# Attention projections of a two-layer transformer kernel in three full blocks, with moved odd heads and transposed values

## The chip, the core and the metric

The kernel runs on one core of a Trainium2 chip. The metric is the time of one execution on the device, in microseconds (us); lower is better. The engines are TensorE (PE, with its weight loads as PEld), VectorE (DVE), ScalarE (ACT), GpSimd (POOL) and SyncE (SP), which issues DMAs here.

## What is computed

x holds 32 batches of 256 tokens with 256 features. A first layer passes each batch through an expert of a conditional feed-forward, then attention, then a top-2 mixture of 8 experts; a second layer follows (base projection with LoRA, shared and routed experts). The change lies in the attention:

```python
def _gqa(x, wq, wk, wv, wo):                      # x is RMS-normed
    q = (x @ wq.T).reshape(B, S, N_HEADS, HEAD_DIM)      # 16 heads of 16
    k = (x @ wk.T).reshape(B, S, N_KV_HEADS, HEAD_DIM)   # 4 heads
    v = (x @ wv.T).reshape(B, S, N_KV_HEADS, HEAD_DIM)   # 4 heads
    k, v = jnp.repeat(k, n_rep, axis=2), jnp.repeat(v, n_rep, axis=2)
    attn = jnp.einsum('bqhd,bkhd->bhqk', q, k) * scale
    attn = jax.nn.softmax(jnp.where(causal, attn, -jnp.inf), axis=-1)
    out = jnp.einsum('bhqk,bkhd->bqhd', attn, v).reshape(B, S, C)
    return out @ wo.T
```

## The kernel before

The kernel is a row of phases: the conditional feed-forward (to about 330 us), the attention with the routing (to about 1055), the sorted experts, LoRA and shared experts, top-k and the routed experts. The engines meet through semaphores only; each engine's list is written out by hand and runs in order.

`attention_phase` runs `body(i)` once per batch on each engine, i from -3 to 31, with a loop of four bodies for batches 8 to 27. A body holds work of several batches: normalised rows of batch i + 3, projections of batch i + 2 (keys, values, queries), scores for the row maxima of batch i + 1, turned scores and exponentials of batch i, the output of batch i - 1 and the residual, the router's logits (`gate`) and, in even iterations, the prefix sums of batches before that (`prefix`).

Every fp32 product is made of three, from high and low parts (`exact_product`, L59 to L61). The projections write two PSUM banks. `piece_a` and `piece_b` are each shared by a fixed ring of users (`A_ORDER`, `B_ORDER`): the user named next may start when the one before it has been emptied, counted in `a_free` and `b_free`. For this change: `piece_b` goes from `kv` to `route` to `shift_q1` to `out_t`; `piece_a` from `heads_q1` to `q_a` to `q_b` to `values_q0`.

Queries and keys lie transposed: `q_t` has 128 partitions, 32 for each of four key groups, and four columns of heads j. Of each 32 rows row 0 holds the shift (minus the maximum, written there by SP with `move_shift`), rows 1 to 16 the head, the rest zeros. `k_t` is laid out alike, with ones in row 0, so that a product of 32 rows gives score minus maximum. The padding makes the queries four blocks of 128 weight columns and the keys a fifth. Each block takes 2 x 3 products over 256 tokens. The values are made untransposed, with tokens on the partitions: 8 products of 128 or 64 columns with `wv`.

In an iteration TensorE goes: turned scores 0, output projection, `turn_max` 0, scores 0, transposes of the norm, values of q1, turned scores 1, transposes of h, `heads` 0, scores 1, `heads` 1, `keys_values`, `queries` q_a, turned scores 2, (`prefix`), `gate`, `queries` q_b, `turn_max` 1 (L1600), scores 2, `turn_out`, values of q0. VectorE takes the maxima of each score bank (L1043), and `divide` frees piece_a for the queries. `keep_kv` copies keys and values (L1079, L1082) out of piece_b, and `keep_q` the first query block. ScalarE takes exponentials (L926), and its `keep_q` copies the second query block.

## Time and profile before

| | |
|---|---|
| median of 3 runs | 2264.63 us (2261.69 to 2268.38) |
| the profiled execution | 2275.81 us |
| its span | 2274.2 us |
| TensorE busy over the span | 2108.6 us (93%) |
| VectorE busy | 1372.2 us (60%) |
| ScalarE busy | 1113.6 us (49%) |
| GpSimd busy | 972.6 us (43%) |

The page has one profiled execution. A busy TensorE is not TensorE at its peak: matmuls are pipelined, and in the order of time the start of the next instruction, not the length of one, says how fast the list goes. An idle stretch stands in square brackets with what ended it.

### The profile page before, as it was taken

How to read it: one execution, taken by the hardware profiler on the slowest of the kernel's cores; microseconds unless marked ns; L12 is line 12 of the kernel's file. 1: busy time of each engine (PE TensorE's matmuls, PEld its weight loads, DVE VectorE, ACT ScalarE, POOL GpSimd, SP SyncE). 2: the span in 40 equal slices, each digit the busy share in tenths (PEclk: the TensorE clock that was granted, in tenths of full speed). 3: DMA queues.
4: the chain of work that ended last, by engine and by line, in shares of the span. 5: the costliest groups of instructions: out<-in, count | busy, mean ns of one | idle time of the engine just before them, and what ended most of it. 6: DMA issues, size and time to landing. Idle time of an engine off the chain costs nothing. (4 is left out here: it accounts for less than half of the span.)

```text
span 2274.2 us, 51155 instructions
## 1 busy us (share of the span) xinstructions
PE 2108.6 (93%) x16904; PEld 1793.8 (79%) x16904; DVE 1372.2 (60%) x2834; ACT 1113.6 (49%) x2206; POOL 972.6 (43%) x1062
## 2 busy tenths in 40 slices
PE   5999978999999999997997999999839999999997
PEld 5999975666666666664996999999828888888886
DVE  5888854576666766676553666666554544444442
ACT  5666643455555555554663333333224544445442
POOL 0000012244554545544654454545235566655653
PEclk9999988999999999997997999999969999999998
DMA  6666630221221212213985444444224545455442
GB/s 229 236 236 237 240 116 25 99 72 63 85 81 62 83 60 86 80 54 110 310 294 172 135 152 137 150 141 149 84 92 105 106 98 115 90 109 108 95 88 31
DMA packets 127209, 285.06 MB, mean 125 GB/s; under 512 B 20705, under 2 KB 58338, under 8 KB 120674
## 3 DMA queue, kind: packets, MB, share of 16 engines
q1 hardware_dynamic: 77026, 173.04, 23.1%
q0 software_dynamic: 50048, 110.14, 19.2%
q8 instruction: 94, 1.54, 0.3%
q14 instruction: 41, 0.34, 0.0%
HBM read 187.17 MB, written 95.42 MB: 124 GB/s over the span
## 5 line engine op out<-in xcount | busy, mean ns | idle before, releaser
L1043 DVE TENSOR_REDUCE neg_max<-ring 128x2 f32<-128x512 f32 (+1 forms) x384 | 251.0, 680 | 109.1 <-PE ring L1554 109.1
L814 POOL TENSOR_SCALAR_AFFINE_SELECT weights_diag<-weights_diag 128x512 f32<-128x512 f32 x256 | 155.7, 633 | 323.5 <-ACT weights_diag L926 322.6
L2584 POOL DMA_INDIRECT out<-eo,row_put x128 | 201.2, 1572 | 162.7 <-ACT eo L2649 138.0
L2724 DVE TENSOR_TENSOR ex_hid<-ex_up_ps,gelu 128x512 f32<-128x512 f32 x128 | 86.9, 688 | 173.8 <-ACT gelu L2633 173.8
L2574 POOL DMA_INDIRECT toks<-hs,row_get x128 | 134.8, 1053 | 133.1 <-DVE row_get L2690 97.2
L2021 POOL DMA_INDIRECT picked_rows<-results,lo_row_now x128 | 145.8, 1139 | 56.5 <-issue 29.3
L2633 ACT ACTIVATE gelu<-ex_gate_ps 128x512 f32<-128x512 f32 x128 | 76.2, 596 | 188.7 <-PE ex_up_ps L61 188.7
L926 ACT ACTIVATE weights_diag<-ring 128x512 f32<-128x512 f32 x256 | 138.4, 599 | 35.7 <-PE ring L1570 35.7
L59 PE MATMUL ex_down_ps<-ex_dn_lo,ex_hid_hi 128*128 128x256 f32 x512 | 144.2, 282 | 2.8 <-issue 2.8
L311 POOL DMA_DIRECT2D c<-c_sb x31 | 17.0, 549 | 303.4 <-DVE c_sb L377 303.4
L61 PE MATMUL ex_down_ps<-ex_dn_hi,ex_hid_hi 128*128 128x256 f32 x512 | 143.8, 281 | 0.0
L60 PE MATMUL ex_down_ps<-ex_dn_hi,ex_hid_lo 128*128 128x256 f32 x512 | 143.7, 281 | 0.0
L822 POOL DMA_INDIRECT sorted_rows<-h_sb,row_now x128 | 127.1, 993 | 34.7 <-issue 32.0
L926 ACT ACTIVATE weights_full<-ring 128x512 f32<-128x512 f32 x128 | 67.3, 602 | 127.3 <-PE ring L1570 127.3
L1570 PE MATMUL ring<-q_t,k_t 32*128 32x512 f32 x768 | 112.1, 654 | 14.2 <-DVE neg_max L1043 9.5
L1550 PE MATMUL ring<-k_t,q_t 32*128 32x128 f32 (+1 forms) x2048 | 114.2, 349 | 11.9 <-issue 5.2
L59 PE MATMUL ps_up<-x_lo,ug_hi 128*128 128x256 f32 x256 | 76.3, 298 | 35.7 <-DVE ug_lo L343 22.1
L2068 ACT ACTIVATE ht_hi<-turned 128x512 fp32r<-128x512 f32 x32 | 19.1, 598 | 183.8 <-PE turned L2289 183.8
L1550 PEld LDWEIGHTS ring<-k_t,q_t 32*128 32x128 f32 x2048 | 81.6, 190 | 34.0 <-issue 28.1
L2717 DVE TENSOR_TENSOR ex_xt_lo<-ex_turned,ex_xt_hi 128x512 fp32r<-128x512 f32 x64 | 41.3, 686 | 110.3 <-ACT ex_xt_hi L2627 110.3
L59 PE MATMUL ex_gate_ps<-ex_xt_lo,gu_hi 128*128 128x512 f32 x256 | 104.3, 407 | 1.5 <-DVE ex_xt_lo L2717 1.5
L60 PE MATMUL ex_gate_ps<-ex_xt_hi,gu_lo 128*128 128x512 f32 x256 | 101.4, 396 | 0.0
(366 smaller groups left out, 7731.6 us busy)
## 6 DMA issues: line engine op xcount, KB each, us to landing
ug_raw<-in_w_ug SPq DMA_DIRECT2D x32, 1028.0 KB, 5.0
dn_raw<-in_w_dn SPq DMA_DIRECT2D x32, 640.0 KB, 6.2
q_t<-sorted_rows SPq DMA_DIRECT2D x136, 128.0 KB, 3.3
expert_gu<-in_expert_gu SPq DMA_DIRECT2D x16, 1024.0 KB, 4.8
results<-c0n POOLq DMA_DIRECT2D x33, 256.0 KB
x_raw<-in_x_t SPq DMA_DIRECT2D x32, 256.0 KB, 5.2
c0n<-c SPq DMA_DIRECT2D x32, 256.0 KB, 3.9
c0r<-c SPq DMA_DIRECT2D x32, 256.0 KB
```

The source lines that it names most:

```text
L59: nc.tensor.matmul(out, lhs_hi, rhs_lo, start=start, stop=False)
L60: nc.tensor.matmul(out, lhs_lo, rhs_hi, start=False, stop=False)
L61: return nc.tensor.matmul(out, lhs_hi, rhs_hi, start=False, stop=stop)
L814: nc.gpsimd.affine_select(part, part, [[0, G], [1, P]], ALU.is_ge, 0.0, base=0, channel_multiplier=-1).then_inc(kept_done, 1)
L822: nc.gpsimd.indirect_dma_start(out=sorted_rows, out_offset=to, in_=h_sb[b[1] % 4][:, t, :], in_offset=None).then_inc(scattered[b[1] % 2], 16)
L926: nc.scalar.activation(tile[:, g, :], slot(2 * r, g)[:], ACT.Exp).then_inc(exp_done, 1)
L1043: nc.vector.tensor_reduce(out, src, AX_X, ALU.max, negate=True).then_inc(max_done, 1)
L1550: nc.tensor.matmul(slot(2 * r + 1, g)[:, c * keys:(c + 1) * keys], q_t[n][rows, j, q * P:(q + 1) * P], k_t[n][rows, 0:keys], start=(c == 0 ...
L1570: nc.tensor.matmul(slot(2 * r, g)[:], k_t[n][rows, k * P:(k + 1) * P], q_t[n][rows, :, q * P:(q + 1) * P], start=True, stop=True).then_inc ...
L2021: nc.gpsimd.indirect_dma_start(out=picked[par][:, n, :], out_offset=None, in_=results, in_offset=bass.IndirectOffsetOnAxis(ap=row_now[par] ...
L2574: nc.gpsimd.indirect_dma_start(out=toks[c][:, n, :], out_offset=None, in_=hs_rows, in_offset=bass.IndirectOffsetOnAxis(ap=at, axis=0)).the ...
L2584: nc.gpsimd.indirect_dma_start(out=out_rows, out_offset=bass.IndirectOffsetOnAxis(ap=at, axis=0), in_=eo[c][:, n, :], in_offset=None, comp ...
```

## The change

The padding goes. The two heads of a pair share a block: rows 0 to 15 of each 32 hold an even head, rows 16 to 31 the odd one, so the queries are two blocks, and the third block holds the keys (rows 0 to 15) and the values (rows 16 to 31).

- ScalarE copies the query bank into the even columns of `q_t`. SP then moves the odd heads with four DMAs from rows 16 to 31 of the even columns to rows 0 to 15 of the odd ones (`move_odd_heads`), and `scores` of the next iteration waits for them. Later the shift is written to row 16 instead of row 0, over the old odd heads.
- ScalarE copies keys and values to `kv_t` in SBUF (`take_kv`). VectorE makes `k_t` from it (times 1 for key rows, plus 1 in row 16, with `of_key`). TensorE turns `kv_t` with two transposes into piece_b (`turn_v`), and VectorE copies the values out (`keep_v`). `v_t` is a new user of piece_b between `kv` and `route`.
- `queries` runs once and is one user of piece_a. The block that stood between `gate` and `turn_max` 1 is gone.
- `scores` uses 16 rows of each group, the turned scores 17. The maps of weights change to fit, and the sorted phase gets two buffers of its own for the parts that lay in the wider weight tiles.

```diff
-VW = NKV * HD
+HALF = 2 * HD
+KV = G // 2
...
-        self.wqk_raw = sb("wqk_raw", [P, KT, G + 1, P])
-        self.wqk_hi = sb("wqk_hi", [P, KT, G + 1, P], F32R)
-        self.wqk_lo = sb("wqk_lo", [P, KT, G + 1, P], F32R)
-        self.wv_raw = sb("wv_raw", [P, KT, VW])
-        self.wv = sb("wv", [P, KT, 2 * VW], F32R)
+        self.wqk_raw = sb("wqk_raw", [P, KT, KV + 1, P])
+        self.wqk_hi = sb("wqk_hi", [P, KT, KV + 1, P], F32R)
+        self.wqk_lo = sb("wqk_lo", [P, KT, KV + 1, P], F32R)
+        self.of_key = sb("of_key", [P, 2])
...
-                    nc.scalar.activation(at.wqk_hi[:, t, 0:G], at.wqk_raw[:, t, 0:G], ACT.Copy, scale=at.norm_q[:, t:t + 1]).then_inc(at.w_hi_done, 1)
-                    nc.scalar.activation(at.wqk_hi[:, t, G], at.wqk_raw[:, t, G], ACT.Copy, scale=at.norm[:, t:t + 1]).then_inc(at.w_hi_done, 1)
-                    nc.scalar.activation(at.wv[:, t, 0:VW], at.wv_raw[:, t], ACT.Copy, scale=at.norm[:, t:t + 1]).then_inc(at.w_hi_done, 1)
+                    nc.scalar.activation(at.wqk_hi[:, t, 0:KV], at.wqk_raw[:, t, 0:KV], ACT.Copy, scale=at.norm_q[:, t:t + 1]).then_inc(at.w_hi_done, 1)
+                    nc.scalar.activation(at.wqk_hi[:, t, KV], at.wqk_raw[:, t, KV], ACT.Copy, scale=at.norm[:, t:t + 1]).then_inc(at.w_hi_done, 1)
...
-        A_ORDER = (("out_proj", -2, B), ("values_q1", -1, B), ("heads_q0", -1, B), ("heads_q1", -1, B), ("q_a", 2, B), ("q_b", 2, B), ("values_q0", 0, B))
-        B_ORDER = (("shift_q0", 0, B), ("norm_t", 2, B), ("h_t", -2, B), ("kv", 2, B), ("route", -2, B + 1), ("shift_q1", 1, B), ("out_t", -1, B))
+        A_ORDER = (("out_proj", -2, B), ("values_q1", -1, B), ("heads_q0", -1, B), ("heads_q1", -1, B), ("q", 2, B), ("values_q0", 0, B))
+        B_ORDER = (("shift_q0", 0, B), ("norm_t", 2, B), ("h_t", -2, B), ("kv", 2, B), ("v_t", 2, B), ("route", -2, B + 1), ("shift_q1", 1, B), ("out_t", -1, B))
...
             def move_shift(b, q):
                 sp.wait_ge(b_free, per_b(f"shift_q{q}", later(b, -q)) + 1)
-                sp.dma_start(q_t[b[1] % 4][0:P:32, :, q * P:(q + 1) * P], shift[q][:]).then_inc(shift_in[q], 16)
+                sp.dma_start(q_t[b[1] % 4][HD:P:32, :, q * P:(q + 1) * P], shift[q][:]).then_inc(shift_in[q], 16)
+
+            def move_odd_heads(i):
+                n = (i[1] + 2) % 4
+                sp.wait_ge(a_free, per_a("q", i) + 1)
+                for g in range(NKV):
+                    sp.dma_start(q_t[n][32 * g:32 * g + HD, 1:G:2, :], q_t[n][32 * g + HD:32 * g + HALF, 0:G:2, :]).then_inc(odd_heads_in, 16)
...
                 if exists(later(i, 4)):
                     load_to_normalise(later(i, 4))
+                if exists(later(i, 2)):
+                    move_odd_heads(i)
                 if exists(later(i, 1)):
                     move_shift(later(i, 1), 1)
...
             def keep_q(i):
-                act.wait_ge(queries_done, times(2, i, 6))
-                nc.scalar.activation(q_t[(i[1] + 2) % 4][:, 2:4, :], piece_a[:].rearrange("p (j s) -> p j s", j=2), ACT.Copy).then_inc(a_free, 1)
+                act.wait_ge(queries_done, times(1, i, 3))
+                nc.scalar.activation(q_t[(i[1] + 2) % 4][:, 0:G:2, :], piece_a[:].rearrange("p (j s) -> p j s", j=2), ACT.Copy).then_inc(a_free, 1)
+
+            def take_kv(i):
+                act.wait_ge(kv_done, times(1, i, 3))
+                until(act, k_t_done, times(1, i, 2))
+                until(act, v_t_done, times(1, i, 2))
+                nc.scalar.activation(kv_t[:], piece_b[:, 0:S], ACT.Copy).then_inc(b_free, 1)
...
                     exps(i, 2, (0, 1))
                 if even(i) and exists(later(i, -4)):
                     second_odds(later(i, -4))
+                if has_next:
+                    take_kv(i)
                 if has:
                     exps(i, 2, (2, 3))
+                if has_next:
+                    keep_q(i)
                 if exists(later(i, 1)):
                     keep_shift(i)
...
-            def keep_kv(i):
-                n = (i[1] + 2) % 4
-                dve.wait_ge(kv_done, times(1, i, 3))
-                nc.vector.tensor_scalar(k_t[n][:], piece_b[:, 0:S], one_rows[:], None, ALU.add)
-                both = piece_b[:, S:512].rearrange("p (t a g d) -> p t g d a", t=TT, a=2, g=NKV)
-                for t in range(TT):
-                    part = nc.vector.tensor_reduce(v[n][:, t, :, 0:HD], both[:, t], AX_X, ALU.add)
-                part.then_inc(b_free, 1)
-
-            def keep_q(i):
-                dve.wait_ge(queries_done, times(2, i, 5))
-                nc.vector.tensor_copy(q_t[(i[1] + 2) % 4][:, 0:2, :], piece_a[:].rearrange("p (j s) -> p j s", j=2)).then_inc(a_free, 1)
+            def keep_k(i):
+                dve.wait_ge(b_free, per_b("kv", i) + 1)
+                nc.vector.scalar_tensor_tensor(out=k_t[(i[1] + 2) % 4][:], in0=kv_t[:], scalar=at.of_key[:, 0:1], in1=at.of_key[:, 1:2].broadcast_to([P, S]),
+                                               op0=ALU.mult, op1=ALU.add).then_inc(k_t_done, 1)
+
+            def keep_v(i):
+                dve.wait_ge(v_t_done, times(1, i, 3))
+                nc.vector.tensor_copy(v[(i[1] + 2) % 4][:, :, :, 0:HD],
+                                      piece_b[:, 0:S].rearrange("p (t g c) -> p t g c", t=TT, g=NKV)[:, :, :, HD:HALF]).then_inc(b_free, 1)
...
                     maxima(s, 1, 1)
-                if has_next:
-                    keep_kv(i)
                 if picks:
                     scaled_gap(m_pick)
-                if has_next:
-                    keep_q(i)
                 if has_scores:
                     maxima(s, 1, 2)
+                if has_next:
+                    keep_k(i)
+                if has_scores:
                     maxima(s, 1, 3)
+                if has_next:
+                    keep_v(i)
...
                     ring_free(times(12, i, 12), times(12, i, 2))
-                    until(pe, b_free, per_b("kv", later(i, -1)) + 1)
+                    until(pe, k_t_done, times(1, i, 2))
+                    pe.wait_ge(odd_heads_in, times(16 * NKV, i, 2 * 16 * NKV))
                 elif r == 1:
                     ring_free(times(12, i, 16), times(12, i, 6))
-                    until(pe, a_free, per_a("q_b", later(i, -1)) + 1)
...
-                        rows = slice(32 * g, 32 * g + 32)
+                        rows = slice(32 * g, 32 * g + HD)
...
-                    rows = slice(32 * g, 32 * g + 32)
+                    rows = slice(32 * g, 32 * g + HD + 1)
...
             def keys_values(i):
                 take_b("kv", i)
                 for k in range(KT):
-                    exact_product(nc, piece_b[:, 0:S], (at.wqk_hi[:, k, G, :], at.wqk_lo[:, k, G, :]),
-                                  (nt_hi[:, k, :], nt_lo[:, k, :]), k == 0, k == KT - 1)
+                    last = exact_product(nc, piece_b[:, 0:S], (at.wqk_hi[:, k, KV, :], at.wqk_lo[:, k, KV, :]),
+                                         (nt_hi[:, k, :], nt_lo[:, k, :]), k == 0, k == KT - 1)
+                last.then_inc(kv_done, 1)
+
+            def turn_v(i):
+                take_b("v_t", i)
                 for t in range(TT):
-                    toks = slice(t * P, (t + 1) * P)
-                    c = S + t * 2 * VW
-                    beside(piece_b[:, c:c + 2 * VW], VW, (nt_hi, nt_lo), toks, at.wv, True)
-                    last = beside_last(piece_b[:, c:c + 2 * VW], VW, (nt_hi, nt_lo), toks, at.wv)
-                last.then_inc(kv_done, 1)
+                    last = nc.tensor.transpose(piece_b[:, t * P:(t + 1) * P], kv_t[:, t * P:(t + 1) * P], at.ident[:])
+                last.then_inc(v_t_done, 1)
...
-            def queries(i, name, heads_):
-                take_a(name, i)
-                for c, j in enumerate(heads_):
+            def queries(i):
+                take_a("q", i)
+                for c in range(KV):
                     for k in range(KT):
-                        last = exact_product(nc, piece_a[:, c * S:(c + 1) * S], (at.wqk_hi[:, k, j, :], at.wqk_lo[:, k, j, :]),
+                        last = exact_product(nc, piece_a[:, c * S:(c + 1) * S], (at.wqk_hi[:, k, c, :], at.wqk_lo[:, k, c, :]),
                                              (nt_hi[:, k, :], nt_lo[:, k, :]), k == 0, k == KT - 1)
                 last.then_inc(queries_done, 1)
...
                     keys_values(i)
-                    queries(i, "q_a", (0, 1))
+                    queries(i)
                 if has:
                     turned_scores(i, 2)
+                if has_next:
+                    turn_v(i)
                 if picks:
                     prefix(i)
                 if has_h:
                     gate(i, not picks)
-                if has_next:
-                    queries(i, "q_b", (2, 3))
...
-    q_rows = np.zeros((G, NKV, 32, D), np.float32)
-    q_rows[:, :, 1:HD + 1] = a[F0 + "wq"].reshape(NKV, G, HD, D).swapaxes(0, 1)
-    k_rows = np.zeros((1, NKV, 32, D), np.float32)
-    k_rows[0, :, 1:HD + 1] = a[F0 + "wk"].reshape(NKV, HD, D)
+    q_rows = a[F0 + "wq"].reshape(NKV, KV, HALF, D).swapaxes(0, 1)
+    kv_rows = np.concatenate([a[F0 + "wk"].reshape(1, NKV, HD, D), a[F0 + "wv"].reshape(1, NKV, HD, D)], 2)
+    in_block = np.arange(P) % 32
...
-        "w_qk": by_rows(np.concatenate([q_rows, k_rows], 0).reshape(-1, D)).reshape(P, KT, G + 1, P),
-        "w_v": by_rows(a[F0 + "wv"]).reshape(P, KT, VW),
+        "w_qk": by_rows(np.concatenate([q_rows, kv_rows], 0).reshape(-1, D)).reshape(P, KT, KV + 1, P),
+        "of_key": np.stack([in_block < HD, in_block == HD], 1).astype(np.float32),
```

TensorE's list, an odd iteration, from the third turned scores on, before (nine more products of the second query block and then the transposed maxima, L1600, follow the last row):

```order
L1570 MATMUL ring<-q_t,k_t 128x512 x3
L1644 MATMUL piece_b<-gate,at_ht_hi 128x16 [waits b_free]
L1645 MATMUL piece_b<-gate,at_ht_lo 128x8
L1649 MATMUL piece_b<-gate,at_ht_lo 128x8
L1650 MATMUL piece_b<-gate,at_ht_hi 128x16
L1644 MATMUL piece_b<-gate,at_ht_hi 128x16
L1645 MATMUL piece_b<-gate,at_ht_lo 128x8
L1649 MATMUL piece_b<-gate,at_ht_lo 128x8
L1650 MATMUL piece_b<-gate,at_ht_hi 128x16
L59 MATMUL piece_a<-nt_lo,wqk_hi 128x256 [waits a_free]
L60 MATMUL piece_a<-nt_hi,wqk_lo 128x256
L61 MATMUL piece_a<-nt_hi,wqk_hi 128x256
```

and after the change:

```order
L1583 MATMUL ring<-q_t,k_t 128x512 x3
L1653 MATMUL piece_b<-at_ident,kv_t 128x128 [waits b_free]
L1653 MATMUL piece_b<-at_ident,kv_t 128x128
L1658 MATMUL piece_b<-gate,at_ht_hi 128x16 [waits b_free]
L1659 MATMUL piece_b<-gate,at_ht_lo 128x8
L1663 MATMUL piece_b<-gate,at_ht_lo 128x8
L1664 MATMUL piece_b<-gate,at_ht_hi 128x16
L1658 MATMUL piece_b<-gate,at_ht_hi 128x16
L1659 MATMUL piece_b<-gate,at_ht_lo 128x8
L1663 MATMUL piece_b<-gate,at_ht_lo 128x8
L1664 MATMUL piece_b<-gate,at_ht_hi 128x16
L1613 MATMUL piece_b<-at_ident,neg_max 16x128 [waits max_done,b_free]
```

The second query block is gone from between the gate's products and the transposed maxima, and two transposes of kv_t stand before the gate, which now waits for them to leave the bank.

ScalarE's list in the same place, before, from the exponentials of the third turned scores (weights_full) on:

```order
L926 ACTIVATE weights_full<-ring 128x512 [waits at_turned_done0]
L926 ACTIVATE weights_full<-ring 128x512 [waits at_turned_done1]
L926 ACTIVATE weights_full<-ring 128x512 [waits at_turned_done2]
L926 ACTIVATE weights_full<-ring 128x512 [waits at_turned_done3]
L954 ACTIVATE shift<-piece_b 16x128 [waits max_t_done]
L950 ACTIVATE q_t<-piece_a 128x512 [waits queries_done]
```

and after:

```order
L937 ACTIVATE weights_full<-ring 128x512 [waits at_turned_done0]
L937 ACTIVATE weights_full<-ring 128x512 [waits at_turned_done1]
L967 ACTIVATE kv_t<-piece_b 128x256 [waits v_t_done,k_t_done,kv_done]
L937 ACTIVATE weights_full<-ring 128x512 [waits at_turned_done2]
L937 ACTIVATE weights_full<-ring 128x512 [waits at_turned_done3]
L961 ACTIVATE q_t<-piece_a 128x2x256 [waits queries_done]
L971 ACTIVATE shift<-piece_b 16x128 [waits max_t_done]
```

The copy to kv_t came in behind the second exponential, and the copy to q_t, which now takes the even columns, stands ahead of the shift.

VectorE's list in the same place, before, from the second maximum of the second score set on:

```order
L1043 TENSOR_REDUCE neg_max<-ring 128x2 [waits scores_done]
L1079 TENSOR_SCALAR k_t<-piece_b,one_rows 128x256 [waits kv_done]
L1082 TENSOR_REDUCE v<-piece_b 128x4x16 x2
L1087 COPY q_t<-piece_a 128x512 [waits queries_done]
L1043 TENSOR_REDUCE neg_max<-ring 128x2 [waits scores_done] x2
L1158 TENSOR_REDUCE logits<-piece_b 128x16 [waits gate_done]
```

and after:

```order
L1062 TENSOR_REDUCE neg_max<-ring 128x2 [waits scores_done] x2
L1097 SCALAR_TENSOR_TENSOR k_t<-kv_t,of_key 128x256 [waits b_free]
L1062 TENSOR_REDUCE neg_max<-ring 128x2 [waits scores_done]
L1102 COPY v<-piece_b 128x8x16 [waits v_t_done]
L1174 TENSOR_REDUCE logits<-piece_b 128x16 [waits gate_done]
L1062 TENSOR_REDUCE neg_max<-ring 128x4 [waits scores_done] x2
```

The copy of the first query block is gone; the keys follow one maximum later and the value copy behind the next.

## Rows read from the trace of the kernel before

**Rows 1.** Stages: busy us and instructions per engine, granted clock, DMA share, GB/s.

```profile
700.00:800.00 100.00, 97.24 (x931) 66.13 (x925) 65.30 (x179) 55.80 (x133) 52.00 (x67) 0.98 0.24 78
```

**Rows 2.** TensorE in order of time (start, us, instruction), an odd iteration.

```profile
703.91 0.36 PE L59 MATMUL piece_b<-nt_lo,wqk_hi 128*128 128x256 f32 x1
...
704.70 0.22 PE L1644 MATMUL piece_b<-wv,nt_hi 128*128 128x128 f32 x1
...
705.54 0.33 PE L59 MATMUL piece_a<-nt_lo,wqk_hi 128*128 128x256 f32 x1
...
707.11 1.14 PE L1570 MATMUL ring<-q_t,k_t 32*128 32x512 f32 x8
...
708.18 0.28 PE L1644 MATMUL piece_b<-gate,at_ht_hi 128*128 128x16 f32 x1
...
708.98 0.26 PE L1650 MATMUL piece_b<-gate,at_ht_hi 128*128 128x16 f32 x1
...
710.59 0.27 PE L1600 MATMUL piece_b<-at_ident,neg_max 128*16 128x128 f32 x1
```

**Rows 3.** The same view, the even iteration that follows.

```profile
731.92 1.14 PE L1570 MATMUL ring<-q_t,k_t 32*128 32x512 f32 x8
...
732.99 0.19 PE L1675 MATMUL piece_b<-chosen,earlier 128*128 128x32 bf16 x1
...
733.99 0.26 PE L1650 MATMUL piece_b<-gate,at_ht_hi 128*128 128x16 f32 x1
...
735.60 0.27 PE L1600 MATMUL piece_b<-at_ident,neg_max 128*16 128x128 f32 x1
```

**Rows 4.** VectorE in order of time: the second division of each iteration.

```profile
704.48 0.42 DVE L1059 TENSOR_TENSOR o<-piece_a,rinv 128x256 f32<-128x256 f32 x1
...
729.65 0.41 DVE L1059 TENSOR_TENSOR o<-piece_a,rinv 128x256 f32<-128x256 f32 x1
```

**Rows 5.** ScalarE in order of time: exponentials of the third turned scores.

```profile
708.26 2.07 ACT L926 ACTIVATE weights_full<-ring 128x512 f32<-128x512 f32 x4 [3.94 <-PE ring L1570]
...
734.14 1.09 ACT L926 ACTIVATE weights_full<-ring 128x512 f32<-128x512 f32 x2
```

**Rows 6.** Groups by line and shape, 600 to 950 us: busy us, mean ns, idle before.

```profile
L1043 DVE TENSOR_REDUCE neg_max<-ring 128x2 f32<-128x512 f32 x128 | 83.6, 677 | 3.6 <-PE ring L1554 3.6
...
L906 ACT ACTIVATE squares<-c0n 128x256 f32<-128x256 f32 x32 | 13.4, 418 | 0.5
...
L1047 DVE COPY shift<-piece_b 16x128 f32<-16x128 f32 x16 | 4.3, 269 | 0.0
```

**Rows 7.** All engines in order of time, iteration 30, which has no next batch.

```profile
1037.50 0.36 PE L1650 MATMUL piece_b<-gate,at_ht_hi 128*128 128x16 f32 x1
...
1038.25 0.38 PE L1600 MATMUL piece_b<-at_ident,neg_max 128*16 128x128 f32 x1 [0.39 <-DVE logits L1158]
```

**Rows 8.** TensorE in order of time, second preparing iteration, 354 to 366 us.

```profile
354.69 0.56 PE L59 MATMUL piece_b<-nt_lo,wqk_hi 128*128 128x256 f32 x1
...
364.10 0.41 PE L1600 MATMUL piece_b<-at_ident,neg_max 128*16 128x128 f32 x1
```

**Rows 9.** All engines in order of time: the kernel's first matmul.

```profile
22.08 0.55 PE L59 MATMUL ps_up<-x_lo,ug_hi 128*128 128x256 f32 x1 [22.08 <-DVE ug_lo L343]
```

**Rows 10.** All engines in order of time: a move of the shift that was waited for.

```profile
1049.06 0.53 SPq L719 DMA_DIRECT2D q_t<-shift  x1
...
1050.88 0.71 PE L1570 MATMUL ring<-q_t,k_t 32*128 32x512 f32 x4 [0.19 <-DMA q_t<-shift]
```

**Rows 11.** TensorE in order of time: two first pieces after the loop's jump back.

```profile
716.20 1.90 PE L1570 MATMUL ring<-q_t,k_t 32*128 32x512 f32 x8 [1.84 <-DVE neg_max L1043]
...
720.36 0.27 PE L1600 MATMUL piece_b<-at_ident,neg_max 128*16 128x128 f32 x1
...
805.21 1.14 PE L1570 MATMUL ring<-q_t,k_t 32*128 32x512 f32 x8 [1.75 <-DVE neg_max L1043]
...
807.78 0.27 PE L1600 MATMUL piece_b<-at_ident,neg_max 128*16 128x128 f32 x1
```

More of the change, by code:

```diff
@@ L1435, in _ @@
             nc.vector.memset(done_of[:], 0.0).then_inc(ones_done, 1)
-            dve.wait_ge(ones_done, 4)
-            for g in range(NKV):
-                nc.vector.memset(one_rows[32 * g:32 * g + 1, :], 1.0).then_inc(ones_done, 1)
-            dve.wait_ge(ones_done, 4 + NKV)
+            dve.wait_ge(ones_done, 3)
             dve.wait_ge(set_done, 9)
```

29 lines of the change are left out of this document (15 added, 14 removed).

## The prediction

> **What bounds the kernel now.** I read the table of stages first, then the order of work on each engine inside one batch. In the attention stage TensorE is busy 97 us of each 100 and VectorE 65 [rows 1]. Within one steady iteration TensorE's rows follow each other without an idle bracket [rows 2, 3]: from the keys-and-values block at 703.91 to the transposed maxima at 710.59 nothing waits. So TensorE's own list sets the pace there, and whatever is taken off it counts in full, unless a wait comes in its place. The other engines wait for it.
>
> Names for what follows: K is the start of the keys-and-values block, T the start of the third turned scores (L1570), M the start of the transposed maxima (L1600). In an odd iteration T is K + 3.20 and M is T + 3.48, in an even one M is T + 3.68 [rows 2, 3]; the even one carries the prefix sums before the gate.
>
> **What the change takes off TensorE.** The eight value products go: 704.70 to 705.54, 0.84 us. Twelve of the 24 query products go: the second block ran from about 709.1 to 710.59, 1.5 us, while the first, 705.54 to 707.11, 1.57 us, stays and now makes all four heads [rows 2]. Two 128-column transposes come in; I take 0.38 us for them with the last one's latency (a single transposed piece shows 0.27, and pieces follow each other at about 0.12, like the six of the keys between 703.91 and 704.70 [rows 2]). If nothing waited, an iteration would be 2.0 us shorter. That is the case for the change.
>
> **The waits that come in.** There are three new handoffs in the same stretch, and the block that covered two of them is the second query block that is removed.
>
> First, the queries now follow the keys at once, at K + 0.79, but piece_a is free only when VectorE's second division has ended: 704.48 + 0.42 is K + 0.99, and in the even case 729.65 + 0.41 is 731.92 - 3.20 + 1.34 [rows 2 to 4]. The value products had covered that. With 0.1 us of handoff (my estimate; the 0.39 of rows 7 holds two short VectorE operations as well) the queries start at K + 1.09 (odd) or K + 1.44 (even), and T comes at K + 2.66 or K + 3.00. So only 0.54 or 0.20 us of the 0.84 is kept.
>
> Second, the transposes of the values need kv_t, and ScalarE makes it behind the first two exponentials of the third turned scores. Those start 1.15 us after T, since 708.26 - 707.11 is 1.15, and four of them take 2.07, so the third place in the list is reached at T + 2.13; in the even iteration the odds come between and the third exponential starts at 734.14, T + 2.22 [rows 2, 3, 5]. The copy is 128x256: between 0.27 (a 16x128 copy on VectorE) and 0.42 (a 128x256 square on ScalarE) [rows 6]; I take 0.38. The transposes start at T + 2.61 or 2.70. TensorE has ended the turned scores at T + 1.14: it is idle 1.5 us, and the copy's keys were ready before T.
>
> Third, the router's products share piece_b and must wait until VectorE has emptied the transposed values, behind the keys and one more maximum: kv_t at T + 2.51, keys 0.35 to the next start, maximum 0.60 to the next start (a row of 0.68 with the overlap off), value copy 0.27, the end at T + 3.73, in the even case 3.82 [rows 6]. The products start 0.1 later. That is another 0.85 us idle. The gate takes 708.98 + 0.26 - 708.18 = 1.06 us, with the prefix sums 733.99 + 0.26 - 732.99 = 1.26 [rows 2, 3]. Then the transposed maxima wait for the logits to leave piece_b. That wait exists today only where no second query block follows: after the products ending at 1037.50 + 0.36 the maxima start at 1038.25, 0.39 us later, in an even iteration [rows 7]; without the row-number addition I take 0.27. So M comes at T + 5.16 (odd) or T + 5.57 (even).
>
> **The sum.** Odd: 2.66 + 5.16 = K + 7.82 against K + 6.68, 1.14 us longer. Even: 3.00 + 5.57 = K + 8.57 against K + 6.88, 1.69 longer. Behind M the list is the same as before, its waits measured from M too, so the difference stays. The mean 1.41 over the 30 iterations that have both the turned scores and a next batch is +42 us. Each handoff could be off by 0.1 to 0.2, so this term lies between +30 and +55.
>
> At the start of the stage there are no exponentials to wait behind. In the second preparing iteration, 354.69 to 364.10 [rows 8], TensorE runs at half clock, 1.6 us of values go and 2.5 of queries with their wait of 0.8, while the transposes and two handoffs bring about 1; the very first batch pays about 1 us more for moving the odd heads before its first scores. Together about -3 us (0 to -5). The first matmul of the kernel waits 22.08 us for a chain in which the attention weights are split [rows 9]; two blocks and the value weights less take between 0 and 2 us off it, and I take -2. This gives +37.
>
> **The moved heads.** Four DMAs of 32 KB go to SP's queue between the loads and the move of shift 1. SP reaches them when ScalarE's copy of the queries ends, about T + 4.05, and a DMA of this queue holds it 0.53 [rows 10]: the last is out at T + 6.2 to 6.4, some 0.3 to 0.5 later than the shift move could have gone (M + 0.6). The shift is wanted 3.7 us after M. In the one row where TensorE waited for such a move it landed 1.82 us after its issue [rows 10]: 0.7 us of cover is left, so I cost it at nothing. If the moves land slower together, the turned scores of the next batch stall. The odd heads themselves are wanted only at the next scores, over 5 us later. The Trainium skill, DMA: Bandwidth & Descriptors, puts a fixed cost of about 2.0 us on a DMA, and the row agrees.
>
> **The clock.** The granted clock is full in this stage [rows 1]. Where TensorE had been idle 1.84 us, it then ran at half: 716.20 to 720.36, 4.16 us, for what took 2.57 after an idle 1.75 us at 805.21 [rows 11]. One fall costs 1.59. The new idle stretches are 1.5, 0.85 and 0.3 us, with only 0.4 and 1.1 us of work between them: the single ones are shorter than the one that brought the fall, the first two together (2.3) longer. I expect a fall in somewhat over half of the iterations, 16 x 1.59 = +25 us; the bounds are 0 and 30 x 1.59 = 48. The Trainium skill, TensorE: Matmul & The Clock Gate, in its part on a second failure mode, says that frequent short idle stretches between groups of matmuls make the gate swing; a reader who took only long single gaps to matter would leave this term out.
>
> By the profiled execution (2275.81 us, span 2274.2), 37 + 25 gives 2338; it is 11 us above the median of the runs, and the same difference on the median 2264.63 gives 2327.
>
> **Rivals.** (a) The waits come, the clock does not fall: 2264.6 + 37 = 2302. For it: 1.75 us idle was borne at 805.21 [rows 11]. (b) The moves of the odd heads delay the shift by a further 1 us each time, so TensorE stalls at the head of every iteration as well: 2327 + 30 = 2357. It decides once the shift lands more than 2.5 us after its issue; the row of 1.82 speaks against it. (c) Faster: scores that use 16 or 17 rows of each group instead of 32 take less. Six sets of scores and turned scores at about 1.1 us each, like the one at 707.11 [rows 2], are some 6.5 us of an iteration; at half of that, 3.2 us would be gained against 1.4 lost, and the time would be 2264.6 - 5 - 54 = 2206. The rows speak against it: 32-row pieces of 512 columns take no less than their columns ask, 0.69 to 1.14 us for the set [rows 2]. It decides above 1.6 us gained in these groups. (d) Part of the waits is not there, because the exponentials or VectorE come to the copies earlier than their places in the lists let me see; at a quarter of the worked-out delay, no clock loss, the time is 2264.6 - 5 + 11, about 2271.
>
> **Numbers.** Forecast, waits and clock: 0.50. (a) 0.24. (b) 0.09. (c) 0.07. (d) 0.10, half of it within 0.3% (7 us, about what a measurement of this kernel can tell), a third faster. So faster 0.10, same 0.06, slower 0.84. The range takes in (a) with its lower handoffs, 2285, less a few us for (d), and the forecast with most of the clock term, up to 2352.
>
> **What would show it.** A transpose of kv_t on TensorE with an idle bracket of about 1.5 us before it, released by ScalarE; one of 0.8 before the router's products, released by VectorE's value copy; 0.3 to 0.4 before the transposed maxima; iterations longer by some 1.4 us, and by up to 3 where the clock falls; a granted clock under full in the stage. No idle bracket before the kv_t transposes would break the forecast, as would score rows shorter than before. A bracket before the turned scores released by the move of the shift speaks for (b), a stage at full clock for (a).

## The result and the profile after

The changed kernel takes 2421.53 us (median of 4 runs, 2420.90 to 2423.88), the kernel before 2263.43 beside it: a ratio of 1.0686, with a 95% interval of 1.0665 to 1.0707. The forecast of "slower" holds. Its size does not: 2327 was given, with 2352 as the upper end, so the loss is 158 us where 62 were reckoned. Here and below ratios are taken over fast runs; one run of e_early (2366.77 us) was in the slower state and does not count.

The table of stages of the changed kernel (columns as in [rows 1]; the number after the five engines is TensorE's granted clock):

```profile
700.00:800.00 100.00, 85.09 (x690) 53.29 (x693) 47.26 (x128) 46.29 (x111) 39.60 (x51) 0.81 0.18 56
500.00:1000.00 500.00, 430.95 (x3514) 268.02 (x3525) 255.61 (x714) 237.10 (x569) 211.56 (x273) 0.83 0.21 65
```

Against [rows 1] TensorE is busy 85 us of 100 and not 97: the waits. The clock is 0.81 and not 0.98: the rest. The granted clock has two levels, 2.4 and 1.2 GHz, so a mean of 0.81 says that 38 of the 100 us ran at the lower.

TensorE in order of time, an even iteration of the changed kernel. It answers to [rows 3], and from the transposed maxima on to the first row after it:

```profile
701.32 1.14 PE L1583 MATMUL ring<-q_t,k_t 17*128 17x512 f32 x8
703.98 0.60 PE L1653 MATMUL piece_b<-at_ident,kv_t 128*128 128x128 f32 x2 [1.52 <-ACT kv_t L967]
705.38 0.21 PE L1689 MATMUL piece_b<-chosen,earlier 128*128 128x32 bf16 x1 [0.80 <-DVE v L1102]
...
705.61 0.36 PE L1658 MATMUL piece_b<-gate,at_ht_hi 128*128 128x16 f32 x1
...
707.10 0.36 PE L1664 MATMUL piece_b<-gate,at_ht_hi 128*128 128x16 f32 x1
707.93 0.38 PE L1613 MATMUL piece_b<-at_ident,neg_max 128*16 128x128 f32 x1 [0.47 <-DVE logits L1174]
708.23 2.09 PE L1563 MATMUL ring<-k_t,q_t 16*128 16x128 f32 x32
...
711.94 1.06 PE L1624 MATMUL piece_b<-at_ident,o 128*128 128x128 f32 x4
712.93 1.75 PE L1604 MATMUL piece_a<-weights_diag,v 128*32 128x512 f32 x8
714.61 0.71 PE L1583 MATMUL ring<-q_t,k_t 17*128 17x512 f32 x4
```

The three brackets are the three waits of the prediction, each with the releaser that it named. After the second one the router's products take 705.61 to 707.10 + 0.36, 1.85 us, where 1.06 was the figure of before, and from the maxima to the next turned scores it is 6.68 us. The stages of these few microseconds show the clock:

```profile
701.30:705.00 3.70, 1.76 (x11) 0.52 (x10) 1.04 (x3) 2.52 (x7) 2.24 (x2) 0.88 0.20 71
705.00:708.00 3.00, 2.16 (x17) 2.07 (x17) 0.61 (x5) 0.39 (x1) 0.00 (x0) 0.50 0.11 22
708.00:714.60 6.60, 6.27 (x48) 3.32 (x49) 2.36 (x6) 1.66 (x4) 0.00 (x0) 0.52 0.05 11
714.60:726.00 11.40, 11.18 (x109) 6.88 (x106) 8.05 (x21) 8.20 (x20) 7.54 (x11) 1.00 0.34 116
```

From about 704 until just before 714.6 the clock is at its lower level, some 10 us, though from 708.2 on TensorE is nearly always busy. What it does there is few-column router products, scores of 128 columns over 16 rows, mask products, transposes and eight value products; below, "light" stands for this stretch without a block of projections (128 rows, 256 columns).

### The profile page after: what moved, and what is told of

It reads as the page before. It is cut to its first block and busy times, and to the rows that moved or that the text cites. A ratio compares the mean times of both kernels' runs of the same rounds, so it can differ in the third digit from the quotient of the medians.

```text
span 2422.3 us, 50275 instructions
## 1 busy us (share of the span) xinstructions
PE 2156.7 (89%) x16296; PEld 1790.7 (74%) x16328; DVE 1340.0 (55%) x2763; ACT 1122.4 (46%) x2236; POOL 970.7 (40%) x1062
## 5 line engine op out<-in xcount | busy, mean ns | idle before, releaser
L1563 PE MATMUL ring<-k_t,q_t 16*128 16x128 f32 (+1 forms) x2048 | 143.2, 424 | 17.2 <-ACT weights_diag L937 7.1
L1563 PEld LDWEIGHTS ring<-k_t,q_t 16*128 16x128 f32 x2048 | 106.3, 255 | 40.7 <-issue 31.5
L1583 PE MATMUL ring<-q_t,k_t 17*128 17x512 f32 x768 | 114.6, 667 | 9.5 <-DMA q_t<-shift 7.6
L61 PE MATMUL ex_gate_ps<-ex_xt_hi,gu_hi 128*128 128x512 f32 x256 | 101.4, 396 | 0.0
```

What stands on the lines that cost most here:

```text
L61: return nc.tensor.matmul(out, lhs_hi, rhs_hi, start=False, stop=stop)
L1563: nc.tensor.matmul(slot(2 * r + 1, g)[:, c * keys:(c + 1) * keys], q_t[n][rows, j, q * P:(q + 1) * P], k_t[n][rows, 0:keys], start=(c == 0 ...
L1583: nc.tensor.matmul(slot(2 * r, g)[:], k_t[n][rows, k * P:(k + 1) * P], q_t[n][rows, :, q * P:(q + 1) * P], start=True, stop=True).then_inc ...
```

## Where the time went

The same two points in both kernels are the transposed maxima of the second preparing iteration and those of iteration 30, both L1613 here and L1600 before. In the changed kernel's order of time, with the first matmul of the kernel and the first transposes of the sorted phase:

```profile
19.00 0.55 PE L59 MATMUL ps_up<-x_lo,ug_hi 128*128 128x256 f32 x1 [19.00 <-DVE ug_lo L342]
...
343.94 2.09 PE L1563 MATMUL ring<-k_t,q_t 16*128 16x256 f32 x16 [4.66 <-DMA q_t<-q_t]
...
357.40 0.28 PE L1613 MATMUL piece_b<-at_ident,neg_max 128*16 128x128 f32 x1 [0.39 <-DVE v L1102]
...
1191.25 0.38 PE L1613 MATMUL piece_b<-at_ident,neg_max 128*16 128x128 f32 x1 [0.39 <-DVE logits L1174]
...
1221.42 1.09 PE L1767 MATMUL ring<-at_ident,q_t 128*128 128x128 f32 x4 [4.92 <-DMA q_t<-sorted_rows]
```

and the last of them in the kernel before:

```profile
1069.29 1.09 PE L1753 MATMUL ring<-at_ident,q_t 128*128 128x128 f32 x4 [5.33 <-DMA q_t<-sorted_rows]
```

| part | before | after | difference | reckoned |
|---|---|---|---|---|
| start to maxima of the second preparing iteration | 364.10 | 357.40 | -6.7 | -5 |
| from there to the maxima of iteration 30 | 674.15 | 833.85 | +159.7 | +42 waits, +25 clock |
| from there to the sorted phase | 31.04 | 30.17 | -0.9 | 0 |
| from there to the end of the span | 1204.9 | 1200.9 | -4.0 | 0 |

The sum is the 148.1 us between the spans, 2422.3 and 2274.2. All of the error stands in the second line.

TensorE's waits over 500 to 1000 us (total us, times, longest):

```profile
PE piece_b L1653 <- ACT kv_t L967: 26.6, 18, 1.5
PE piece_b L1689 <- DVE v L1102: 8.4, 9, 1.0
PE piece_b L1658 <- DVE v L1102: 7.9, 9, 0.9
PE piece_b L1613 <- DVE logits L1174: 7.2, 18, 0.5
...
PE piece_a L59 <- DVE o L1078: 2.3, 6, 0.5
```

Per iteration these are 1.48, 0.91 and 0.40 us, against 1.5, 0.85 and 0.3 to 0.4 in the prediction. The queries wait 0.4 us in six iterations, fewer than worked out for the second division; the step from the keys to the third turned scores takes 2.66 us in the odd iterations, as forecast, and 2.67 or 2.97 in most even ones against 3.00. The waits do not explain more than the 42 us; some 117 us, 3.9 per iteration, are left, and in the rows above they are 1.85 - 1.06 for the gate and 6.68 - 3.71 behind the maxima, together 3.8. Over the 30 iterations the stretch behind the maxima takes 5.7 to 6.9 us, 6.5 on average, so one iteration's 3.8 is a little above the mean. (3.71 is 710.59 to the start of the next turned scores in the kernel before.)

## Experiments

All ratios are against the kernel before, run in the same set on the same chip; its median was 2284 us in the first set, 2277, 2265, 2285 and 2281 in the others, so ratios are compared and not times. "Clock" is the mean granted clock from 500 to 1000 us; the kernel before has 1.00 there. e_nomove, e_rows32, e_fill and e_kvfirst rest on two runs each.

| run | what differs | ratio (95%) | clock |
|---|---|---|---|
| c_after | the changed kernel once more | 1.0699 (1.0669 to 1.0730) | 0.82 |
| e_nomove | without the four moves | 1.0599 (1.0524 to 1.0673) | 0.83 |
| e_b17 | the kernel before, 17 rows | 1.0075 (1.0054 to 1.0096) | 0.99 |
| e_rows32 | 32 rows | 1.0468 (1.0431 to 1.0505) | 0.90 |
| e_fill | work in the 1.5 us wait | 1.0472 (1.0425 to 1.0520) | 0.90 |
| e_fill32 | both | 1.0385 (1.0361 to 1.0409) | 0.95 |
| e_fill_late | that work behind the gate | 1.0796 (1.0758 to 1.0835) | 0.87 |
| e_kvfirst | kv_t copied first on ScalarE | 1.0378 (1.0334 to 1.0422) | 0.90 |
| e_early | kv_t, keys and values early | 1.0359 (1.0292 to 1.0426) | 0.90 |
| e_early32 | the same, 32 rows | 1.0233 (1.0202 to 1.0264) | 0.96 |
| e_order | e_early, shift first | 0.9970 (0.9948 to 0.9992) | 0.94 |
| e_order32 | the same, 32 rows | 0.9860 (0.9831 to 0.9889) | 0.99 |
| e_split | early, shift first, queries split | 0.9878 (0.9841 to 0.9914) | 0.99 |
| e_split32 | the same, 32 rows | 0.9813 (0.9793 to 0.9832) | 0.99 |

### Without the moves of the odd heads

```diff
-                if exists(later(i, 2)):
-                    move_odd_heads(i)
```

e_nomove leaves the four DMAs out, so half of the heads are zero.

> The changed kernel without the four DMAs per batch that move the odd heads (the odd columns of the query tiles stay zero, so half of the heads are wrong); the scores wait for the copy of the queries instead. Idle theory: within 5 us of 2421, since the moves end under other work. Move theory: at least 30 us less, and the turned scores at the head of an iteration start earlier after the transposed maxima.

The ratio is 1.060, a seventh of the loss below c_after's 1.070, with intervals that just overlap. It lies between the two theories. The profiled execution is the slower of its two (2424.74 us, 1.061 of the kernel before beside it); in it the clock is 0.83, and the wait before the transposes is the same, again 18 times. The turned scores do not start earlier after the maxima either: 6.5 to 6.9 us in most iterations, as in the changed kernel. So the moves are not what makes the loss; whether they cost 0.01 of it is not settled.

```profile
PE piece_b L1655 <- ACT kv_t L968: 26.6, 18, 1.5
```

> The changed kernel itself, as the yardstick for the others on this chip. Its ratio to the kernel before was 1.069; the same is expected here.

Run again on the second set's chip, the changed kernel gave the same ratio and clock.

### Fewer rows, with and without the waits

```diff
-                        rows = slice(32 * g, 32 * g + 32)
+                        rows = slice(32 * g, 32 * g + HD + 1)
```

for e_b17 (in the kernel before, in scores and turned scores), and in the changed kernel the other way for e_rows32, with `q_t` filled with zeros at the start.

> The kernel before, with scores and turned scores reading 17 rows of each group of 32 instead of all 32 (the rest are zeros). Idle theory and move theory: no change, 2264, full clock in the attention stage. Narrow-rows theory: the clock falls in the stage and the time rises by 50 us or more. If narrow pieces were shorter, 2206.

> The changed kernel with all 32 rows of each group read by scores and turned scores (the query tiles are zeroed once at the start; scores then hold a foreign term, so the output is not the reference's). Idle theory: 2420, clock 0.82 in the stage. Narrow-rows theory: the clock recovers, 2310 or less.

The two answers differ, and neither theory holds whole. In the kernel before, which has long waits only at the loop's jumps, reading 17 rows costs 17 us (0.0075) where none was expected, and the clock is 0.99. TensorE's sum of waits there has 4.5 us for `ot_sb` in 16 short ones, which the kernel before does not show; how the rows bring them is not known. Where the waits are, going back to 32 rows wins 0.023, a third of the loss, with the waits unchanged. TensorE in e_rows32:

```profile
605.26 0.44 PE L1657 MATMUL piece_b<-at_ident,kv_t 128*128 128x128 f32 x2 [1.43 <-ACT kv_t L970]
...
608.00 0.27 PE L1617 MATMUL piece_b<-at_ident,neg_max 128*16 128x128 f32 x1 [0.36 <-DVE logits L1178]
608.20 1.82 PE L1567 MATMUL ring<-k_t,q_t 32*128 32x128 f32 x32
...
611.63 0.77 PE L1628 MATMUL piece_b<-at_ident,o 128*128 128x128 f32 x4
612.33 1.06 PE L1608 MATMUL piece_a<-weights_diag,v 128*32 128x512 f32 x8
```

The fall comes here too, but the transposes at 611.63 already take 0.77 and not 1.06, and the values at 612.33 run at full speed. So with these waits the fall does not need the narrower pieces; they keep the clock down longer. (Behind a single short wait they also decide whether it falls, as e_order shows below.) They are no shorter either: eight turned scores take 1.14 us with 17 rows (701.32) and with 32 [rows 2]. That settles rival (c).

### Work in place of the wait

```diff
                 if has_next:
+                    queries(i, again=True)
                     turn_v(i)
```

The query products are made a second time, 1.5 us of 128-row products, where TensorE was idle for 1.5 us.

> The changed kernel, with the twelve query products of each batch made a second time, into the same bank, between the third turned scores and the transposes of kv_t; the copy of the queries waits for the second pass. The products do nothing new; they stand where TensorE was idle for 1.5 us. Idle theory (the long half-clock stretches come from the idle stretches around the kv_t transposes): the order and the two later waits stay, the clock falls in few iterations, and the time comes to 2264 + 1.4 x 30, about 2305, at most 2340. Narrow-rows theory (TensorE's clock falls because scores now use 16 rows of each group): the clock is as low as in the changed kernel, 0.82 in the stage, and the time stays at 2420 or above. Move theory (four DMAs per batch are what costs): 2420 as well.

> The changed kernel with both suspects of the clock taken away together: the query products are made a second time between the third turned scores and the transposes of kv_t (no idle there), and the scores and turned scores read 32 rows of each group instead of 16 and 17. The router's products and the transposed maxima still wait 0.88 and 0.36 us, and the second making costs 1.5 us where 1.4 us were idle. If each of the two only shortens the stretch at half clock by its own share (201 us with the filler, 177 with the rows, 328 with neither): about 60 us of half clock are left, and the ratio is 1.02 to 1.025. If the two remaining waits are enough for a fall in each iteration whatever stands around them: half clock stays above 150 us and the ratio stays above 1.035. If the clock is full all through, only the waits remain, 1.4 us in each of 30 iterations, and the ratio is 1.015 to 1.02.

More work, and the kernel is faster than the changed one: 1.047 against 1.070 with 17 rows. The clock goes from 0.82 to 0.90 though TensorE's list is longer by these products. It is not the 2340 us at most (1.034) that I had put on it: falls remained in many iterations. With 32 rows as well it is 0.95, and each step helps where the other is already made (1.0472 to 1.0385). But 1.0385 is far above the 1.02 to 1.025 that I had expected if the two shares just add up. The 0.9 and 0.4 us waits are left in it and still bring falls, though not in each iteration:

```profile
603.19 0.28 PE L1662 MATMUL piece_b<-gate,at_ht_hi 128*128 128x16 f32 x1 [0.88 <-DVE v L1106]
...
604.61 0.27 PE L1617 MATMUL piece_b<-at_ident,neg_max 128*16 128x128 f32 x1 [0.36 <-DVE logits L1178]
604.81 2.09 PE L1567 MATMUL ring<-k_t,q_t 32*128 32x128 f32 x32
...
627.92 0.19 PE L1695 MATMUL piece_b<-chosen,earlier 128*128 128x32 bf16 x1 [0.95 <-DVE v L1106]
...
629.63 0.27 PE L1617 MATMUL piece_b<-at_ident,neg_max 128*16 128x128 f32 x1 [0.47 <-DVE logits L1178]
629.92 1.17 PE L1567 MATMUL ring<-k_t,q_t 32*128 32x128 f32 x32
```

The 32 scores at 604.81 take 2.09 us, the time of the lower clock (1.17 at the full one), after a wait of 0.88 and one of 0.36 alone. One iteration on, waits of 0.95 and 0.47 brought no fall. Of the 20 iterations from 500 to 1000 us 15 take 5.2 us or more from the maxima to the next turned scores, and five take 3.7 to 3.8, as at the full clock. So the lengths of the waits alone do not say whether the clock falls.

> The changed kernel with the query products made a second time, as in e_fill, but between the router's products and the transposed maxima, where the second query block stood before the change. The waits of 1.5 and 0.85 us before the transposes and the router's products stay, the one of 0.4 is covered, and 1.5 us of work comes in for it, so at an unchanged clock the iteration is 1.1 us longer than the changed kernel's. If the long idle stretches alone bring the falls and set their length: half clock 300 us or more, and a ratio of 1.08 to 1.10, above the changed kernel's 1.07. If it is the missing block of 128-row products between the light ones that lets the clock stay low, the half clock is halved (100 to 200 us) and the ratio is 1.045 to 1.06 in spite of the added work; at full clock all through it would be 1.034.

e_fill_late has the same work between gate and maxima, where the second query block stood. Its ratio is at the lower edge of the first case and its clock between the two; it brought a wait of its own: ScalarE's copy of the queries comes later, SP's four moves behind it, the shift last. Its waits over 500 to 1000 us:

```profile
PE piece_b L1653 <- ACT kv_t L967: 25.1, 17, 1.5
PE ring L1583 <- DMA q_t<-shift: 18.1, 13, 2.9
```

The clock rose from 0.82 to 0.87 with both long waits still there. The price was 1.1 us of net work and 1.0 us (18.1 over 17 iterations) of the new wait. So a dense block behind the waits helps the clock but does not decide it.

### The wait taken out by order

```diff
+                if has_next:
+                    take_kv(i)
                 if has:
                     exps(i, 2, (0, 1))
...
-                if has_next:
-                    take_kv(i)
```

> The changed kernel with ScalarE's copy to kv_t ahead of the exponentials of the third turned scores instead of behind two of them. Idle theory: the transposes follow the turned scores at once, so 1.5 us of idle goes per iteration (45 us in all), and the products after them wait only for VectorE. The one long idle stretch is gone, so most falls of the clock go as well: 2300 or less if none is left, relative to 2264 for the kernel before. If two waits of 0.9 and 0.4 us still bring the fall: 1.069 - 0.020 = 1.049. If the kv_t wait were not the trigger: the same clock as the changed kernel.

With no work added, moving ScalarE's copy ahead of the exponentials wins 0.032 over c_after (1.0699 to 1.0378). Nearly half of the loss hung on the place of one copy of 0.39 us. It is not the 2300 us that I had put on a kernel without falls: the clock is 0.90, and what is left waits for VectorE.

e_early also has VectorE make the keys before two of the maxima and copy the values one maximum earlier, and TensorE turn them before the third turned scores.

> The changed kernel with the same work in another order: ScalarE copies kv_t before the exponentials, VectorE makes the keys before the maxima and copies the values one place earlier, and TensorE turns the values before the third turned scores. The queries stay in one block behind the keys. Two of the three waits go, the one before the transposed maxima (0.4 us, behind the logits) and the one for the second division stay. If short waits close together bring the falls: the clock is above 0.95 of full, the iteration is about 20.6 to 21.4 us against 21.4 before, and the ratio is 0.975 to 1.0. If TensorE falls each time that light products (router, transposed maxima) follow one another with a single wait of 0.3 to 0.4 in them: clock below 0.93, ratio 1.02 to 1.04.

> The same reordering with 32 rows of each group read. If reading 32 rows keeps the clock up as it did with the split queries (0.981 against 0.988): 0.005 to 0.01 below the reordering alone. If the reordering alone already has the full clock: no difference, within 0.003.

Two of three waits are gone, and with 17 rows nothing clear is won over e_kvfirst (1.0359 against 1.0378, intervals that overlap); with 32 rows it is 1.0233. A new wait had come that neither expectation names. All engines in order of time in e_early32:

```profile
648.47 0.63 ACT L964 ACTIVATE q_t<-piece_a 128x512 f32<-128x512 f32 x1
648.94 0.25 ACT L974 ACTIVATE shift<-piece_b 16x128 f32<-16x128 f32 x1
...
649.12 2.64 SPq L729 DMA_DIRECT2D q_t<-q_t  x4
...
654.21 1.25 PE L1587 MATMUL ring<-q_t,k_t 32*128 32x512 f32 x8 [2.56 <-DMA q_t<-shift]
```

and the sum over 500 to 1000 us:

```profile
PE ring L1587 <- DMA q_t<-shift: 42.9, 21, 2.6
```

The shift was ready at 649.2, but SP was issuing the four moves until 651.8. TensorE waits 2.0 us in each iteration. This is rival (b)'s mechanism. Behind the wait of 2.56 the clock fell, too (0.50 from 656 to 658). In the changed kernel SP does this:

```profile
705.42 2.63 SPq L728 DMA_DIRECT2D q_t<-q_t  x4
708.63 0.60 SPq L722 DMA_DIRECT2D q_t<-shift  x1
```

There the maxima start 6.61 us after the third turned scores (701.32 to 707.93), when the moves are nearly out, and the shift goes 0.70 us behind them. In e_early32 the maxima start at 647.87, 2.49 us after the turned scores at 645.38, but the queries are copied only at 649.10: the moves, which had stood before the maxima, now stand behind them. So it is the waits taken out in front of the maxima that uncovered the queue. I sent the shift first, on ScalarE and on SP:

```diff
                 if exists(later(i, 1)):
                     move_shift(later(i, 1), 1)
+                if exists(later(i, 2)):
+                    move_odd_heads(i)
```

> e_early with the shift first: ScalarE copies the shift before the queries, and SP moves it before the four moves of the odd heads, so that the 1 to 2.7 us wait of TensorE for the shift goes. It differs from e_split only in that all query products stand behind the keys and none between the router's products and the transposed maxima, where the wait of 0.36 to 0.47 us for the logits stays. If a single wait of 0.4 us and a light stretch without dense products in it bring no fall: clock 0.97 or more, ratio 0.99 to 1.0 (e_split was 0.988; 0.4 + 0.2 us more of waits in 30 iterations is 0.008). If the light stretch with that wait in it brings the falls by itself: clock 0.93 or less and a ratio of 1.01 to 1.03.

> The same with 32 rows of each group read. If the rows add to a fall and don't make one: e_order's clock is below full and this one's is 0.98 or more, with a ratio of 0.985 to 0.995. If the falls come from the wait alone, the two agree within 0.005 and lie above 1.01. The 1.9 to 2.7 us wait for the shift of e_early32 should be gone from the chain: about 60 us, or 0.026, below e_early32's 1.023 if no new wait comes.

The wait for the shift is gone, and both are faster than the kernel before: 0.997 and 0.986. This edit alone is worth 0.037 to 0.039 against e_early and e_early32, more than the wait itself, since falls go with it. e_order32 still has its wait before the maxima, and no dense block between router and maxima:

```profile
PE piece_b L1617 <- DVE logits L1178: 9.6, 24, 0.5
```

Its clock is 0.99. With 17 rows the same list is at 0.94: from the maxima to the next turned scores it takes 5.2 to 6.8 us in 10 of 22 iterations from 500 to 1000 us and 3.7 in the others; with 32 rows one of 24 takes more than 3.7. So one short wait and the light stretch behind it are borne with 32 rows and not always with 17.

### The version with the queries split

e_split is e_order with the second half of the query products between gate and maxima; the bank is large enough for both halves, so only TensorE's list changes.

> A version that keeps the three blocks but puts work into each wait: kv_t copied before the exponentials, the first query block, the transposes, the third turned scores, the gate, and only then the second query block; the shift is copied and moved before the queries. Idle theory: no wait over 0.5 us, full clock, and the transposed maxima come 1.4 to 1.8 us earlier than before in each iteration: 2264 - 48 - 5, about 2211, ratio 0.977. Narrow-rows theory: clock falls remain, ratio above 1.0. If the late moves of the odd heads hold the scores: a wait there released by the move, and part of the gain is lost.

> The version with work in each wait, and with all 32 rows of each group read by scores and turned scores (zeroed tiles; a term that is the same for all keys of a query is added to its scores and leaves the softmax as it is). If the rows matter only after a fall of the clock, and none is left, the same as with 16 and 17 rows. If 32 rows keep the clock up where small waits remain, up to 20 us less.

e_split gains less than the 0.977 expected; the step from 17 to 32 rows, 0.0065, is within what was expected. e_split32 takes 2235.30 us against 2277.11, 0.9813 of the kernel before. One iteration of its TensorE list:

```profile
713.45 0.27 PE L1617 MATMUL piece_b<-at_ident,neg_max 128*16 128x128 f32 x1
...
717.15 1.14 PE L1587 MATMUL ring<-q_t,k_t 32*128 32x512 f32 x8
...
730.61 0.38 PE L1657 MATMUL piece_b<-at_ident,kv_t 128*128 128x128 f32 x2
...
733.70 0.27 PE L1617 MATMUL piece_b<-at_ident,neg_max 128*16 128x128 f32 x1
```

None of the three handoffs has a bracket. Maxima to next turned scores take 3.70 us, the figure of before, and this iteration 20.25 us. Of the 2.0 us that the prediction put at "if nothing waited" 1.4 are reached (42 us over 30 iterations). The waits view has 10.3 us for exponentials and `ot_sb` from 500 to 1000 us, some 0.4 per iteration, and 0.2 are not accounted for.

## Why the prediction was right and wrong

**Right: the work saved and the waits, in kind and size.** The copy to kv_t takes 388 ns (0.38 taken), the value copy 281 (0.27). The three waits came where and as long as worked out. The start gave 6.7 us against 5; in it the first scores waited 4.66 us for the odd heads, while the first matmul came 3.1 us earlier, not 2.

**Wrong: the clock's term.** It was a count times a price, and both failed. The count: 16 falls of 30. The single idle stretches were each shorter than the 1.84 us that had brought a fall in [rows 11], and I kept that as the measure. In the changed kernel the clock is low at the scores behind the maxima in all 30 iterations, and in e_fill32 it fell after 0.88 and 0.36 us in most. The price: 1.59 us, from the turned scores at 716.20 to the maxima at 720.36 [rows 11]. There the output projection follows, 128-row products of 256 columns, and the price is whole: the clock was back at 720.4. I carried it to a place where light work follows. There the fall costs 3.8 us by the rows above, 0.8 before the maxima and 3.0 behind them. With 30 x 3.8 = 114 for the clock the sum is 2264.6 + 37 + 114 = 2416, against 2421.5; the 3.8 is read from the result, so this only checks that little else is missing.

The trace of before had held nearly that price. In iteration 30, where no second query block follows [rows 7], the clock had fallen after the loop's jump:

```profile
1033.79 2.04 PE L1570 MATMUL ring<-q_t,k_t 32*128 32x512 f32 x8 [1.76 <-DVE neg_max L1043]
...
1036.01 0.36 PE L1644 MATMUL piece_b<-gate,at_ht_hi 128*128 128x16 f32 x1
...
1038.57 2.09 PE L1550 MATMUL ring<-k_t,q_t 32*128 32x128 f32 x32
...
1044.66 0.71 PE L1570 MATMUL ring<-q_t,k_t 32*128 32x512 f32 x4
```

and the stages there and in a steady iteration:

```profile
1036.00:1044.60 8.60, 8.21 (x64) 5.17 (x60) 2.39 (x8) 2.85 (x7) 0.00 (x0) 0.53 0.01 3
710.60:714.30 3.70, 3.70 (x51) 1.95 (x48) 1.55 (x3) 2.14 (x5) 0.00 (x0) 1.00 0.03 7
720.40:724.00 3.60, 3.60 (x43) 1.92 (x40) 3.12 (x14) 1.27 (x3) 2.82 (x4) 1.00 0.11 14
```

The last row is the one behind the output projection of [rows 11]. Iteration 30 has the very stretch that the change makes: gate, a wait of 0.39, maxima, scores. 1038.25 to 1044.66 is 6.41 us at the lower clock, 2.7 more than 3.71, and the gate takes 1.85 us and not 1.06: 3.5 in all. I had read from it only the bracket. It was also shown before that 1.76 us could bring a fall and 1.75 (805.21) not, so that no single length was a safe measure.

**The rivals.** (a), waits without a fall, is refuted: the clock is 0.81 to 0.83. (b) is not what happened in the changed kernel: the shift goes 0.70 us behind the maxima, where "M + 0.6" was the earliest. It comes in e_early32, where the maxima stand ahead of the moves. My 0.53 us per move was low, 2.60 to 2.64 us for four and not 2.1. (c) is refuted, 17 rows take the time of 32, and they harm in a way that no rival had; the 0.69 us given there "for the set" is the time of one piece, a set takes 1.14. (d) is refuted by the waits view.

**Open.** Why pieces of 16 and 17 rows keep the clock down longer is shown as a fact (e_rows32, e_order32) and not explained, nor why they let it fall more often in e_order. Which of two like pairs of waits brings a fall (e_fill32) is open too. What e_fill_late would give without its new wait was not measured.

The Trainium skill, TensorE: Matmul & The Clock Gate, in its part on a second failure mode, had warned that frequent short idle stretches make the gate swing. The trace agrees, with a clock of 0.82 from waits of 1.48, 0.91 and 0.40 us per iteration; what it costs had to be read from rows, and I had read too few of them.

## What to carry to other kernels

Work taken off the busiest engine is a gain only if what was behind it is ready: list each handoff that the removed block covered, and reorder the producers (here one copy, two vector operations and five DMAs) in the same edit. That turned 1.070 into 0.997 here; 32 rows and split queries made it 0.981. Cost a fall of the clock by the whole stretch until rows run at full speed again, in the place where it will happen; in this kernel it was more than twice as dear before light work as before the output projection (3.8 and 1.59 us). After one wait is taken out, look for the next: the maxima came 4 us earlier against the turned scores, and a queue that had been harmless cost 2 us per iteration.

## What had not been expected of the hardware

- The granted clock fell in 15 of 20 iterations in which the long wait was gone and waits of 0.9 to 1.0 and 0.4 to 0.5 us were left, with little more than 1 us of light work between them (e_fill32), while a single wait of 1.75 us was borne [rows 11].
- The clock stayed at the lower level for about 10 us in which TensorE was busy most of the time (0.50 from 705 to 708 and 0.52 from 708 to 714.6), while the work was few-column products, 16-row scores, mask and value products and transposes.
- Products that read 16 or 17 rows of a group of 32 take the same time (1.14 us for eight), cost 0.0075 in the kernel before, and make the kernels with waits 0.009 to 0.023 slower than 32 rows do (e_fill32 least, e_rows32 most).
- Adding 1.5 us of products per iteration in an idle stretch made the kernel 0.023 faster (e_fill against c_after).
- Four DMAs of 32 KB inside SBUF hold SP's queue 2.64 us.
